# Neighbour products of a block-banded mixing matrix at half height, a narrower mix matrix, and byte planes in the decode

## What is computed

```python
attn = jnp.einsum('ds,td->st', w1, w2) * sparse_mask        # 1024 x 1024
y = jax.nn.gelu(jnp.einsum('bds,st->bdt', x, attn) + b2, approximate=False)
x = _layernorm(x + y, axis=-1)                              # x: (4, 512, 1024)
mask = jnp.linalg.norm(x, axis=-1) > 64.0
w_l = dequant_kbit(qweight, lut4, 4)                        # (1024, 1024) by 4-bit codes
w_h = dequant_kbit(qweight, lut8, 8)
y = jnp.where(mask[..., None], x @ w_h.T, x @ w_l.T) + bias
x = _layernorm(x + y, axis=-1)
```

## Time and profile before

| | us |
|---|---|
| runs of the kernel | 334.88, 335.72, 339.28 (median 335.72) |
| span of the profiled execution | 336.6 |
| PE / ACT / DVE / POOL busy | 311.2 / 203.5 / 212.5 / 109.7 |
| first matmul of the mix matrix | 9.2 |
| first matmul after the last one of the mix matrix | 58.3 |
| first matmul of the linear part | 121.8 |
| last full stretch of PE ends | 320.7 |

### The profile page before, as it was taken

How to read it: one execution, slowest core, us unless ns; L and a number is a source line. 1 busy time by engine, 2 the same in 40 slices (tenths; PEclk the granted TensorE clock), 3 DMA queues, 4 the chain that set the end, 5 groups by cost and what they waited for, 6 DMA issues and landing times.

```text
span 336.6 us, 5284 instructions
## 1 busy us (share of the span) xinstructions
PE 311.2 (92%) x1979; PEld 281.6 (84%) x1979; DVE 212.5 (63%) x390; ACT 203.5 (60%) x264; POOL 109.7 (33%) x185
## 2 busy tenths in 40 slices
PE   4999897899988979999999999999999999999970
PEld 1989796688766879999999989999999888888870
DVE  3697789649599276699696767756324345534361
ACT  5456984799987974794967849494414344121210
POOL 1000101122149531596788710100513333322210
PEclk9999997999999979999999999999999999999996
DMA  7986584999970892010110100111614686444232
GB/s 284 341 291 202 196 213 79 357 328 262 187 125 2 141 204 61 20 47 18 47 49 23 41 32 33 49 47 64 248 44 145 225 261 237 164 149 157 93 127 72
DMA packets 24754, 47.69 MB, mean 142 GB/s; under 512 B 2320, under 2 KB 9360, under 8 KB 24720
## 3 DMA queue, kind: packets, MB, share of 16 engines
q1 hardware_dynamic: 20368, 38.87, 33.0%
q0 software_dynamic: 4352, 8.39, 14.2%
HBM read 34.67 MB, written 12.58 MB: 140 GB/s over the span
## 4 chain that ended last, share of the span: by engine, by line
PE 41%; ACT 18%; POOL 14%; issue 11%; DVE 10%; DMA 4%; SPq 0%; POOLq 0%; ACTq 0%; DVEq 0%
PE acc L428 10%; PE acc L430 10%; PE acc L429 10%; ACT leaf L596 7%; PE acc L361 7%; POOL cols L1169 4%; DMA w_stage<-in_w2b 4%; ACT z L576 3%; DVE leaf L843 3%; POOL cols L1176 3%; POOL cols L1187 2%; POOL cols L1172 2%; ACT zz L640 1%; ACT dest L596 1%; DVE dest L843 1%
## 5 line engine op out<-in xcount | busy, mean ns | idle before, releaser
L428 PE MATMUL acc<-lin,zz 128*128 128x256 f32 (+2 forms) x424 | 130.9, 309 | 1.8 <-POOL lin L1234 1.8
L430 PE MATMUL acc<-lin,zz 128*128 128x256 f32 (+2 forms) x424 | 130.5, 308 | 0.0
L429 PE MATMUL acc<-lin,zz 128*128 128x256 f32 (+2 forms) x424 | 130.3, 307 | 0.0
L428 PEld LDWEIGHTS acc<-lin,zz 128*128 128x128 f32 x424 | 80.7, 190 | 6.1 <-issue 2.0
L430 PEld LDWEIGHTS acc<-lin,zz 128*128 128x128 f32 x424 | 80.8, 191 | 4.1
L429 PEld LDWEIGHTS acc<-lin,zz 128*128 128x128 f32 x424 | 80.9, 191 | 4.0
L596 ACT ACTIVATE leaf<-planes,lut,flip 128x1024 f32<-128x1024 uint16 x56 | 67.4, 1239 | 0.2
L843 DVE COPY_PREDICATED leaf<-planes,leaf 128x1024 f32<-128x1024 uint16 x32 | 43.7, 1365 | 22.1 <-ACT leaf L596 21.3
L1224 POOL DMA_DIRECT2D z<-in_xt x16 | 19.5, 1270 | 82.8 <-ACT z L576 82.8
L710 ACT ACTIVATE junk<-rows,cols 128x1024 bf16<-128x1024 f32 x15 | 17.2, 1150 | 43.4 <-POOL cols L1198 43.4
L843 DVE COPY_PREDICATED dest<-planes,leaf 128x1024 f32<-128x1024 uint16 x24 | 32.8, 1366 | 15.9 <-ACT leaf L596 11.0
(11 more groups left out here) (87 smaller groups left out, 454.2 us busy)
## 6 DMA issues: line engine op xcount, KB each, us to landing
z<-in_xt SPq DMA_DIRECT2D x16, 512.0 KB, 8.8
z<-in_xt POOLq DMA_DIRECT2D x16, 512.0 KB, 8.0
out_rows<-rows SPq DMA_DIRECT2D x15, 512.0 KB, 2.9
w_stage<-in_w2b SPq DMA_DIRECT2D x8, 512.0 KB, 5.5
w_stage<-in_w1b SPq DMA_DIRECT2D x8, 512.0 KB, 5.3
out_rows<-parts SPq DMA_DIRECT2D x32, 128.0 KB, 1.9
rows<-out_rows SPq DMA_DIRECT2D x16, 256.0 KB, 2.7
band<-in_mask SPq DMA_DIRECT2D x6, 192.0 KB, 2.9
```

The costliest lines, as they stand in the source:

```text
L428: nc.tensor.matmul(bank, hi, w_hi, start=k == 0, stop=False)
L429: nc.tensor.matmul(bank, hi, w_lo, start=False, stop=False)
L430: last = nc.tensor.matmul(bank, lo, w_hi, start=False, stop=k == KB - 1)
```

## The change

- x, w1, w2 and the mask come to the chip in natural feature order, so that the band reaches at most 72 places (REACH) into a neighbour. The mix matrix is made in strips of 72 + 128 + 72 columns (`strip`), 24 matmuls each, from a w2 that is kept whole. Its masking writes, in three pieces, 15 blocks: 8 own blocks and 7 blocks between neighbours, of which the upper half of the partitions serves one side and the lower half the other. The permutation to the order of the planes is done in that write. A second copy of x in permuted order (`xr`) is what POOL adds.
- What of the band lies further than 64 rows from its block (32 rows in all, in six blocks) goes through an extra small product: `excess_strip` makes 96 x 48 values in 8 plain fp32 matmuls, five small DVE instructions place them, and one matmul of 96 rows by 512 columns (`xe`) is added in 6 of 8 units of each group.
- The mix of a group is 8 `own` units of three full-height matmuls, and 7 `beside` pairs. A pair is three times two matmuls of 64 rows: one on partitions 0 to 63 into the bank of block t, one on partitions 64 to 127 into the bank of block t+1.
- w1, w2 pass through three stages instead of two; a load of w1 waits for the strip that used the buffer.
- Planes are bytes: 8 shifts for a block instead of 16, each on pairs of bytes with the mask 0x0101, into two buffers. The row mean is made by DVE instead of POOL.
- The steps are redistributed: two tiles of `z` group 1 are no longer split inside the mix, but in the first linear part; in the last group of the mix, group 0 is. 24 instead of 22 leaves stand ahead of the linear part. The last transpose is moved ahead of the last half.

```diff
+WINDOW, STRIDE, STRIPES = 6, 32, 3
+SIDE = P // 2
+SPAN = STRIDE * (STRIPES - 1)
+BITS = 8
+REACH = -(-(SPAN + WINDOW - 1) // BITS) * BITS
+EDGE = 4
...
+    BYTES = D // BITS
+    LOW_BIT_OF_EACH = 0x0101
+    STRIP = REACH + P + REACH
+    BLOCKS = 2 * KB - 1
...
+    EARLY_STEPS = {2: 2, 3: 3, 4: 4, 5: 4, 6: 4, 7: 4}
+    UNIT_STEPS = [n % 2 for n in range(18)] + [1, 1, 1, 0, 0, 0]
+    FIRST_STEPS = [2] * TILES
+    LAST_MIX_Z = {1: (0, 0), 2: (0, 1), 3: (0, 2), 4: (0, 3)}
+    FIRST_Z = [((1, 0), (1, 1))] + [((1 + n // PAIRS, n % PAIRS),) for n in range(2, 3 * PAIRS)] + [()] * 5
+    SECOND_STEPS = [2] * 15 + [1]
+    BESIDE = (0, 2, 1, 3, 5, 4, 6)
+    HALVES = 2 * len(BESIDE)
...
+                if b >= STAGES:
+                    sp.wait_ge(mix_made, b - STAGES + 1)
+                sp.dma_start(w1_stage[:, b % STAGES, :, :], w1b[b]).then_inc(w1_loaded[b % STAGES], 16)
...
+                    sp.dma_start(w1_e[:, :, :], w1e).then_inc(e_loaded, 16)
+                    sp.dma_start(w2_e[:, :, :], w2e).then_inc(e_loaded, 16)
+                    sp.dma_start(band_e[0:EXCESS, :, :, :], mask_e).then_inc(e_loaded, 16)
+                    load_xe(0)
...
+            def strip(b):
+                first, end = strip_of(b)
+                bank = acc[:, STRIP_BANKS[b % 2], places_of(b)]
...
+                    hi, lo = w1_hi[b % 2][:, d, :], w1_lo[:, b % STAGES, d, :]
+                    nc.tensor.matmul(bank, hi, w2_hi[:, d, first:end], start=d == 0, stop=False)
+                    nc.tensor.matmul(bank, hi, w2_lo[:, d, first:end], start=False, stop=False)
+                    last = nc.tensor.matmul(bank, lo, w2_hi[:, d, first:end], start=False, stop=d == KB - 1)
...
+            def own(g, t):
+                if g:
+                    pe.wait_ge(gelu_done, KB * (g - 1) + t + 1)
+                    if g - 1 in TURN_IN_MIX and t < 2:
+                        pe.wait_ge(lin_lo_made, TURN_IN_MIX[g - 1] + 1)
+                else:
+                    pe.wait_ge(mix_lo_made, t + 1)
+                    if UNIT_BANKS[t] == EXCESS_BANK:
+                        pe.wait_ge(mix_e_step, 4)
+                    if UNIT_BANKS[t] in STRIP_BANKS:
+                        pe.wait_ge(masked, KB)
+                pe.wait_ge(x_lo_made, PAIRS * g + t // 2 + 1)
+                bank, hi, lo = unit_bank(t), mix_hi[:, 2 * t, :], mix_lo[:, 2 * t, :]
+                nc.tensor.matmul(bank, hi, x_hi[:, t, :], start=True, stop=False)
+                nc.tensor.matmul(bank, hi, x_lo[:, t, :], start=False, stop=False)
+                nc.tensor.matmul(bank, lo, x_hi[:, t, :], start=False, stop=False)
+                if t in UNITS:
+                    pe.wait_ge(xe_lo_made, g + 1)
+                    if g == t == 0:
+                        pe.wait_ge(mix_e_step, 4)
+                    nc.tensor.matmul(bank, mix_e[0:EXCESS, UNITS.index(t), :], xe[0:EXCESS, g % 2, :], start=False,
+                                     stop=False)
+
+            def beside(g, t):
...
+                    pe.wait_ge(mix_lo_made, t + 2)
+                pe.wait_ge(x_lo_made, PAIRS * g + (t + 1) // 2 + 1)
+                done = 2 * (1 + BESIDE.index(t))
+                earlier = [u for u in (t - 1, t + 1) if u in BESIDE[:BESIDE.index(t)]]
+                if earlier:
+                    pe.wait_ge(mixed, HALVES * g + halves_for(earlier))
+                for mix, x in ((mix_hi, x_hi), (mix_hi, x_lo), (mix_lo, x_hi)):
+                    ends = [mix is mix_lo and done == halves_for((u - 1, u)) for u in (t, t + 1)]
+                    before = nc.tensor.matmul(unit_bank(t), mix[0:SIDE, 2 * t + 1, :], x[0:SIDE, t + 1, :],
+                                              start=False, stop=ends[0])
+                    after = nc.tensor.matmul(unit_bank(t + 1), mix[SIDE:P, 2 * t + 1, :], x[SIDE:P, t, :],
+                                             start=False, stop=ends[1])
+                before.then_inc(mixed, 1)
+                after.then_inc(mixed, 1)
...
+                for t in (2, 3, 0, 1):
+                    own(g, t)
+                beside(g, 0)
+                beside(g, 2)
+                for t in (4, 5, 6):
+                    own(g, t)
+                beside(g, 1)
+                beside(g, 3)
+                beside(g, 5)
+                own(g, 7)
+                turn_in_mix(g)
+                beside(g, 4)
+                beside(g, 6)
...
+                        if t % 2:
+                            make_x_hi(g + 1, t // 2)
+                        if t == 2:
+                            make_xe_hi(g + 1)
+                    elif t in LAST_MIX_Z:
+                        make_z_hi(*LAST_MIX_Z[t])
...
+                product, wanted = in_bytes(acc[:, STRIP_BANKS[b % 2], 0:STRIP]), in_bytes(band[:, b % 2, :])
+                side, first, end = REACH // BITS, REACH // BITS, (REACH + P) // BITS
+                last = nc.vector.tensor_tensor(by_bit(mix_raw[:, 2 * b, :]), product[:, first:end, :],
+                                               wanted[:, first:end, :], ALU.mult)
+                if b:
+                    last = nc.vector.tensor_tensor(by_bit(mix_raw[0:SIDE, 2 * b - 1, :])[:, P // BITS - side:, :],
+                                                   product[0:SIDE, 0:side, :], wanted[0:SIDE, 0:side, :], ALU.mult)
+                if b + 1 < KB:
+                    last = nc.vector.tensor_tensor(by_bit(mix_raw[SIDE:P, 2 * b + 1, :])[:, 0:side, :],
+                                                   product[SIDE:P, end:, :], wanted[SIDE:P, end:, :], ALU.mult)
+                last.then_inc(masked, 1)
...
-                    last = nc.vector.tensor_scalar(planes[:, :, s * W16:(s + 1) * W16], q16, s, 1,
-                                                   ALU.logical_shift_right, ALU.bitwise_and)
+                    last = nc.vector.tensor_scalar(planes[:, b % 2, :, s * BYTES:(s + 1) * BYTES].bitcast(u16), pairs, s,
+                                                   LOW_BIT_OF_EACH, ALU.logical_shift_right, ALU.bitwise_and)
...
+            def mean_of_row(b):
+                dve.wait_ge(rows_summed, b + 1)
+                nc.vector.tensor_scalar(neg_row_mean[:, b:b + 1], row_sum[:, b:b + 1], 1.0, -1.0 / D, ALU.add,
+                                        ALU.mult).then_inc(row_mean_made, 1)
```

591 lines of the change are left out of this document (325 added, 266 removed).

## The result

The changed kernel takes **352.87 us** (352.07 to 353.92, four runs) against 337.5 us of the kernel before on the same chip (334.88 to 340.17, four runs): ratio **1.047** (95% interval 1.042 to 1.052). It is 4.7% slower; 333.1 us was predicted, with a range to 341.5.

The account below looks back on a forecast made before the run. PE alone was taken to bound the kernel from 121.8 us, so only the linear part's start counted: 119.2 + 214.8 = 334.0 us of span against 336.6, -2.6 on the median 335.7, hence 333.1 us; range 325 to 341.5.

Parts of the forecast that it names:

- Groups 1 to 3: Mix of groups 1 to 3: a loop through PE and ACT sets the period, 13.2 to 14.3 us.
- my ring: Loop between mix groups: PE's 35 slots 7.9 us, ACT 4.1 or 5.2, x_lo 1.2, then the next group's own unit 2.
- I count the same loss once, as before: Half clock after PE's idling before the linear part: the same loss as in the kernel before, counted once.
- the fall in each group: Rival, half clock in the mix: each group's first 4 us slow, loop 2 us longer in three groups, 339; chance 0.08.
- The strips: Mix-matrix stage: DVE is the gate; last strip starts at 58.0, takes 3.0 us, PE done at 61.0.
- The tail: End of the mix, from group 3's pair 1: ACT's chain of GELUs, `zz` splits, leaves and lin takes 12.1 us.
- Pairs and switches: Half-height matmuls in the mix: a pair costs 0.227 us side by side, each height change 0.1 on the loop, 1.3 in all.
- the serial pairs: Rival: the two matmuls of a pair run one after the other, 0.454 us; time 343.7; chance 0.10.
- the full drain: Rival: every change of matmul height costs 0.35 us, 9.1 in all; time 340.9, or 336.4 half hidden; chance 0.14.
- The linear part: From the linear part's start to the end: carried over unchanged at 214.8 us.
- Byte planes: DVE's plane shifts: eight fewer in each of five blocks of the linear part take off 40 x 0.14 us.
- My rival on the slower side: Pairs in the mix run one after the other: linear part starts at 129.8, time 343.7; chance 0.10.

Follow-up runs that it names:

- xe_early: Changed kernel with the load of `xe` for group 2 asked for behind group 2's own x, not behind the x of groups 2 and 3: 348.60 us, 1.032.
- lin0_early: Changed kernel with the split of the first transposed block (`lin_hi`, `lin_lo`) before GELU 4 of group 0 instead of behind GELU 7: 354.33 us, 1.049.
- three_moves: Changed kernel with the edits of xe_early, lin0_early and zz_in_gaps together: 341.37 us, 1.011 of the kernel before.
- four_moves: three_moves with one decode step taken from each of strips 4 and 7, and two put into group 1's first unit: 338.81 us, 1.002.
- keep_clock: Changed kernel with 76 matmuls of 512 columns, whose results nobody reads, added in five places where PE would stand: 350.15 us, 1.037.
- zz_in_gaps: Changed kernel with group 0's four `zz` splits before GELU 1 of groups 2 and 3, not between group 3's last GELUs: 348.59 us, 1.032.
- six_moves: four_moves with own units in order 0 to 3 (groups 2, 3), `xe` behind GELU 0, three leaves moved into the linear part, earlier memsets: 335.09 us, 0.991.
- before_bytes_ones: The kernel before with byte planes and POOL's memsets of ones ahead of group 1's additions, without half-height products: 333.63 us, 0.985.

## Why the prediction was wrong

**The failed step is "Groups 1 to 3", the period of the loop.** It was drawn as 13.2 to 14.3 us, and in the profile the two periods are 23.5 and 18.2 us, because two waits that stood in the program had no price and the half clock had none in this stage. Taken apart, in us:

| | predicted | measured |
|---|---|---|
| end of the strips | 61.0 | 63.7 |
| rest of group 0 | 7.5 | 8.5 |
| group 1 | 13.4 | 23.5 |
| group 2 | 14.1 | 18.2 |
| group 3 to the linear part | 23.2 | 25.0 |
| linear part to the end | 214.8 | 212.8 |

- *Group 1, 10.1 us too short.* Two waits had no price at all. The first is `xe` behind 4 MB of x: I gave its load a cost in the strip stage, and none here, though it was a new step on SP's queue behind eight loads. The second is own unit 0's wait for `lin_lo` of the first block, 3.19 us; it stands in the diff as a condition, and I never asked when ACT and DVE get to it behind GELU 7. They overlap: xe_early alone gives group 2 at 92.4, lin0_early alone nothing, and both with the moved `zz` 87.8. The 15.3 us that are then left between the starts of groups 1 and 2 (72.48 to 87.78 in three_moves) are 1.9 more than my ring. In four_moves it takes as long (69.09 to 84.39): pair 1 is done 9.0 us after the group's start instead of 7.9 (switches, steps, the way to ACT); ACT needs the 4.1 us that I drew; and x_lo 1 comes on DVE behind a merge and `xe`, 2.1 us after x_hi 1 instead of 1.2:

```profile
80.91 1.36 DVE L991 COPY_PREDICATED leaf<-planes,leaf 128x1024 f32<-128x1024 uint8 x1
82.31 0.68 DVE L959 TENSOR_TENSOR xe<-xe_raw,xe 32x512 fp32r<-32x512 f32 x1
83.02 1.23 DVE L964 TENSOR_TENSOR x_lo<-z,x_hi 128x1024 fp32r<-128x1024 f32 x1
```

- *Group 2, 4.1 us too short.* Thirteen matmuls at half clock are 2.6 us of it; the other 1.5 are near the 1.9 that the ring was short above.
- *The clock.* "I count the same loss once, as before" was wrong. The trace of before showed a fall after 1.83 us of idling, and it held a second one that I overlooked: its last strip takes 4.4 us from 53.84 to 58.27, where 24 matmuls of 256 columns at full clock take 2.9. And I had drawn waits of 1 to 5 us for each group. From the last strip on the slow steps sum to 10.0 us: the strip 24 x 0.10, 8, 13 and 9 matmuls of the mix x 0.20, the Gram products 1.6. Two earlier strips (33 to 36 and 43 to 47 us) have some 15 slow steps each besides, 0.10 longer. I had given the fall in each group a chance of 0.08 and 6 us. What the sum costs on the path is not shown: the added matmuls got back 2.7 us in keep_clock, and 0.3 and 0.2 in the repaired kernels, but they also held PE up themselves, as said there.
- *The strips.* DVE as the gate, and the last strip at 58.0, were right (58.47, behind a w_lo that ends at 58.37). It ran at half clock, 5.2 us instead of 3.0, and so ended 2.7 us late. One sum was off by 0.4 us in all: three masking instructions of 0.22 for one of 0.56 are 0.1 more for each strip, not 0.2; measured, the three take 0.82, 0.26 more.
- *The tail.* From pair 1 of group 3 to the end of the last GELU it took 12.2 us (124.49 to 136.7) against 12.1 drawn. Right: the four splits of `zz` stood in that chain with 3.8 us and the three leaves with 3.4. zz_in_gaps bears the splits out, with 6.1 us by the spans and 4.3 by the medians: they had stood in slack before, and could have stayed there. six_moves points the same way for the leaves.
- *Pairs and switches.* A pair costs 0.23 side by side, as taken. A change of height costs 0.1 in the step before and 0.1 in the one behind, 0.2 and not 0.1: 1.3 us more for the changes on the loop. Both rivals fall, the serial pairs (0.45) and the full drain (0.35 for a change). The Trainium skill (TensorE: Matmul & The Clock Gate, Part 3) lets matmuls in distinct row groups start about 4 ns apart; in the changed kernel's trace the two of a pair start 0 to 40 ns apart, nearly all within 10. The Trainium skill (TensorEngine Tiling (Array Packing), Key Properties) says that changing the tiling mode drains TensorE, and gives no price; the trace shows 0.2 us for each change, and whether that is a drain it doesn't tell.
- *The linear part.* Carried over as it stood; 2.0 us less came out. About 1.5 of it is that its first tiles now run at full clock (0.12 instead of 0.21, in 16 steps).
- *Byte planes.* I gave them 0.14 us for each shift off DVE's slack; alone they bring 2.8 us. 1.0 of it may be PE's waits for DVE before transposes, which the trace of before has between 121.8 and 330 and that of before_bytes_ones has not; the rest I can't place.

My rival on the slower side was built on the pairs, the new operation. The loss came from the program around them: a load, the places of the splits and the leaves, and in part the clock. With the waits repaired that I went after, the changed mix, narrow strips and bytes stand at 0.988 to 0.991; the old mix with bytes and an earlier memset at 0.985, 1.5 us less on the same chip. What PE still waits for in the repaired one is DVE's sum in the strip stage (w_lo, up to 5.3 us at once) and the ring between groups (6.9 us for x_lo), in which ACT's wait for `xe` of group 3 (2.1 us) was left. Whether fewer merges in the strip stage or an earlier `xe` would turn the comparison, no run has tried.

## What to carry to other kernels

When a change adds an input, look at what stands ahead of its load on the same queue, and who waits behind its first use: 192 KB behind 4 MB cost 4.3 us here. Where PE was the bound and the change relieves it, write down a ring for each buffer that is used again, with every wait in it, and expect half clock behind each new gap; part of it may be swallowed by a later wait. Matmuls added to hold the clock are no clean test of its price: look whether they outlast the gap. Measure the small by-products of a change alone: the byte planes brought 0.8% by themselves, and the half-height mix, repaired, nothing beyond them that these runs can tell.
